# Loading and transposing 14 of 39 expert tiles in 32x32 blocks on VectorE instead of on TensorE

## What is computed

```
logits = x @ gate_w.T                       # 2048 rows, 8 experts
topk_w, topk_idx = top_k(softmax(logits), 2)   # then normalised to sum 1
h = einsum('th,ehi->eti', x, w1)            # 256 -> 176
g = einsum('th,ehi->eti', x, w3)
y_all = einsum('eti,eih->eth', silu(h) * g, w2)
y = sum of the two chosen experts' rows, weighted by topk_w
shared = silu(x @ sw1) * (x @ sw3) @ sw2    # 256 -> 352 -> 256, every row
```

## Time and profile before

| | us |
|---|---|
| median of 3 runs (lowest, highest) | 730.09 (728.05, 730.45) |
| the profiled execution | 729.91 |
| its span | 727.9 |
| TensorE busy, matmul | 716.8 |
| VectorE busy | 617.2 |
| ScalarE busy | 526.8 |
| GpSimd busy | 506.2 |
| clock granted to TensorE over the span | 0.998 |

### The profile page before, as it was taken

The page is one execution under the profiler, slowest core; times in us unless marked ns, Lnnn a source line. Parts: engine busy times, 40 slices in busy tenths (PEclk is TensorE's granted clock), DMA queues, the critical chain, the costliest instruction groups (busy, mean ns, idle before and its releaser), DMA issues.

```text
span 727.9 us, 16486 instructions
## 1 busy us (share of the span) xinstructions
PE 716.8 (98%) x5490; PEld 690.7 (95%) x5490; DVE 617.2 (85%) x1774; ACT 526.8 (72%) x1664; POOL 506.2 (70%) x531
## 2 busy tenths in 40 slices
PE   7999999999999999999999999999999999999997
PEld 6999999999999999999999999999999989999997
DVE  5888899989998999899989898989898976776657
ACT  5787777777777777777777777777777765666564
POOL 5898467787777777877777777777767623544545
PEclk9999999999999999999999999999999999999999
DMA  6555213221422143214321421131454373344383
GB/s 213 155 176 166 86 31 138 108 88 37 136 106 87 45 135 117 79 46 143 116 77 44 143 106 56 43 103 38 140 205 162 138 270 113 118 123 126 109 292 107
DMA packets 51211, 85.91 MB, mean 118 GB/s; under 512 B 8632, under 2 KB 43416, under 8 KB 49528
## 3 DMA queue, kind: packets, MB, share of 16 engines
q1 hardware_dynamic: 47080, 73.44, 30.3%
q0 software_dynamic: 4048, 11.42, 4.4%
HBM read 60.12 MB, written 44.59 MB: 144 GB/s over the span
## 4 chain that ended last, share of the span: by engine, by line
PE 80%; DVE 8%; POOL 6%; ACT 2%; issue 2%; DMA 1%; SPq 1%; POOLq 0%; DVEq 0%
PE bank L662 60%; PE bank L712 5%; PE bank L702 3%; PE bank L721 3%; POOL work L489 3%; DVE work L1104 2%; POOL rows_by_expert L1917 2%; DVE work L1097 1%; POOL qkt_lo L1788 1%; PE bank L954 1%; PE bank L935 1%; PE bank L704 1%; DVE xn L1261 1%; PE bank L849 1%; ACT work L1553 1%
## 5 line engine op out<-in xcount | busy, mean ns | idle before, releaser
L489 POOL TENSOR_TENSOR work<-work 128x512 f32<-128x512 f32 x127 | 164.9, 1298 | 52.7 <-DVE work L1104 51.9
L1788 POOL TENSOR_TENSOR qkt_lo<-work,qkt_hi 128x512 fp32r<-128x512 f32 x112 | 144.8, 1293 | 74.1 <-ACT qkt_hi L1546 74.1
L1104 DVE TENSOR_TENSOR work<-bank,sinn 64x512 f32<-64x512 f32 x256 | 176.2, 688 | 3.4
L662 PE MATMUL bank<-xnt_hi,w_lo 128*128 128x256 f32 x512 | 148.6, 290 | 0.8 <-DVE xnt_lo L1430 0.8
L662 PE MATMUL bank<-xnt_hi,w_hi 128*128 128x256 f32 x512 | 145.2, 284 | 0.0
L662 PE MATMUL bank<-xnt_lo,w_hi 128*128 128x256 f32 x512 | 145.2, 284 | 0.0
L1546 ACT CAST qkt_hi<-work 128x512 fp32r<-128x512 f32 x112 | 69.6, 622 | 87.3 <-POOL work L489 87.1
L1553 ACT ACTIVATE work<-work,bias 128x128 f32<-128x128 f32 (+1 forms) x256 | 112.7, 441 | 0.9 <-DVE bias L1113 0.9
L1097 DVE TENSOR_TENSOR work<-bank,cosn 128x512 f32<-128x512 f32 x128 | 88.0, 687 | 23.5 <-PE bank L662 23.2
L662 PEld LDWEIGHTS bank<-xnt_hi,w_lo 128*128 128x128 f32 x512 | 98.3, 192 | 1.7 <-DVE xnt_lo L1430 1.0
L662 PEld LDWEIGHTS bank<-xnt_hi,w_hi 128*128 128x128 f32 x512 | 98.6, 193 | 0.5
(11 more groups left out here) (205 smaller groups left out, 2125.3 us busy)
## 6 DMA issues: line engine op xcount, KB each, us to landing
rows_by_expert<-in_zero_t SPq DMA_DIRECT2D x17, 1028.0 KB
weights_split<-stage SPq DMA_DIRECT2D x40, 176.0 KB
w_lo<-weights_split SPq DMA_DIRECT2D x4, 1408.0 KB, 9.7
w_lo<-results_by_token SPq DMA_DIRECT2D x16, 256.0 KB, 5.3
w_lo<-rows_by_expert SPq DMA_DIRECT2D x24, 128.5 KB, 2.1
w_hi<-weights_split SPq DMA_DIRECT2D x2, 1536.0 KB, 6.4
stage<-in_L_ffn_w SPq DMA_DIRECT2D x32, 88.0 KB, 2.2
weights_split<-stage SPq DMA_DIRECT2D x20, 128.0 KB
```

Source lines behind the costliest of these rows:

```text
L489: eng.tensor_tensor(roped[:, a], rope_cos[:, a], rope_sin[:, a], ALU.add).then_inc(rope_add, 1)
L662: mm = pe.matmul(out, lhs[a], rhs[b], start=start and n == 0, stop=stop and n == 2, skip_group_check=more)
L1104: op = nc.vector.tensor_tensor(rope_sin[lo:lo + 64, a], p_qk[a][hi:hi + 64, :, :], sn, ALU.mult)
L1788: nc.gpsimd.tensor_tensor(qkt[a][1][:, :, :], roped[:, a], qkt[a][0][:, :, :], ALU.subtract).then_inc(qkt_lo, 1)
```

## The change

Fourteen tiles are marked in a list `BY_BLOCKS`: 5, 7, 9, 11, and of the tiles from 25 on those whose number is not a multiple of three: 25, 26, 28, 29, 31, 32, 34, 35, 37, 38.

A marked tile is loaded by five transfers instead of one: for each quarter q of the channels (64 of 256) one that puts the tile's rows, in four blocks of 32, on partitions 32q to 32q + 31 (128 pieces of 256 bytes), and one for the last word of each row (128 pieces of 4 bytes). VectorE then transposes the whole 128x256 slot in 32x32 blocks with one instruction into an SBUF buffer `x_turn`, in iteration j - 2, behind `low_x(j-1)`. For a marked tile TensorE has no `turn_x`, and `high_x` and `low_x` read `x_turn` in place of `p_xe`. `high_x` waits for `x_turned` and for `ue_ps` of tile j - 2.

For this the channels stand in another order in all tiles: channel 2s + c on partition s of piece c. The experts' w1 and w3 are loaded in that order (each partition's row is still 704 bytes), and the transposes that stay on TensorE read every second word of the slot.

```diff
@@ constants
+BY_BLOCKS = [j in (5, 7, 9, 11) or j >= NF + 4 and j % 3 > 0 for j in range(NJ)]
@@ buffers
+        x_turn = [work[:, 2560:2560 + D], work[:, 1728:1728 + D]]
+        QW = D // 4
+        def by_channel(row):
+            return row.rearrange("p (s c) -> p c s", c=DC)
+        def got_count(j):
+            return sum(80 if BY_BLOCKS[i] else 16 for i in range(j % ESLOTS, j + 1, ESLOTS))
@@ add_kept of w1 and w3
-                rc = slice(c * P, (c + 1) * P)
-                add_kept([(lambda t: t[:, 0:I], w1[e][rc]), (lambda t: t[:, I:UW], w3[e][rc])], UW,
+                gate, up = (t[e].rearrange("(p c) i -> c p i", c=DC)[c] for t in (w1, w3))
+                add_kept([(lambda t: t[:, 0:I], gate), (lambda t: t[:, I:UW], up)], UW,
@@ tile_in (SyncE)
-                sp.dma_start(x_slot[j % ESLOTS], xs_d[bass.ds(row, P), :]).then_inc(x_got[j % ESLOTS], 16)
+                if BY_BLOCKS[j]:
+                    for q in range(4):
+                        src = xs_d[bass.ds(row, P), q * QW:(q + 1) * QW].rearrange("(k i) s -> i k s", k=4)
+                        sp.dma_start(x_slot[j % ESLOTS][32 * q:32 * q + 32, 0:D].rearrange("p (k s) -> p k s", k=4),
+                                     src).then_inc(x_got[j % ESLOTS], 16)
+                    with nc.allow_non_contiguous_dma(reason="a word of each row"):
+                        sp.dma_start(x_slot[j % ESLOTS][:, D:RW], xs_d[bass.ds(row, P), D:RW]).then_inc(x_got[j % ESLOTS], 16)
+                else:
+                    sp.dma_start(x_slot[j % ESLOTS], xs_d[bass.ds(row, P), :]).then_inc(x_got[j % ESLOTS], 16)
@@ turn_x and its call (TensorE)
-                    mm = pe.transpose(p_xe[:, c, :], x_slot[j % ESLOTS][:, c * P:(c + 1) * P], ident[:, :])
+                    mm = pe.transpose(p_xe[:, c, :], by_channel(x_slot[j % ESLOTS][:, 0:D])[:, c], ident[:, :])
-                if j + 1 < NJ:
+                if j + 1 < NJ and not BY_BLOCKS[j + 1]:
                     turn_x(j + 1)
@@ VectorE
+            def turn_blocks(j):
+                dve.wait_ge(x_got[j % ESLOTS], got_count(j))
+                nc.vector.transpose(x_turn[j % 2].rearrange("p (c k i) -> p k c i", c=DC, k=4),
+                                    x_slot[j % ESLOTS][:, 0:D].rearrange("p (k s c) -> p k c s", k=4, c=DC)).then_inc(x_turned, 1)
             def low_x(j):
+                if BY_BLOCKS[j]:
+                    nc.vector.tensor_tensor(xe_t[1][:, j % 2], x_turn[j % 2].rearrange("p (c s) -> p c s", c=DC), xe_t[0][:, j % 2],
+                                            ALU.subtract).then_inc(xe_lo, 1)
                 if j + 1 < NJ:
                     low_x(j + 1)
+                if j + 2 < NJ and BY_BLOCKS[j + 2]:
+                    turn_blocks(j + 2)
@@ high_x (ScalarE)
+                if BY_BLOCKS[j]:
+                    act.wait_ge(x_turned, turned_by_dve(j))
+                    act.wait_ge(ue_ps, j - 1)
+                    nc.scalar.copy(xe_t[0][:, j % 2], x_turn[j % 2].rearrange("p (c s) -> p c s", c=DC)).then_inc(xe_hi, 1)
```

More of the change, by code:

```diff
@@ L192, in build, with turned_by_dve, turned_by_pe @@
         assert XSLOTS * TOP * D <= rows_at
+        x_turn = [work[:, 2560:2560 + D], work[:, 1728:1728 + D]]
[4 more added lines that the diff above has]
+            return sum(80 if BY_BLOCKS[i] else 16 for i in range(j % ESLOTS, j + 1, ESLOTS))
+        def turned_by_dve(j):
+            return sum(BY_BLOCKS[:j + 1])
+        def turned_by_pe(j):
+            return j + 1 - turned_by_dve(j)
         twin = work[:, DC * P:DC * P + ST * RW].rearrange("p (t d) -> p t d", t=ST)
@@ L336, in build @@
         xe_ps = sem("xe_ps")
+        x_turned = sem("x_turned")
         xe_hi = sem("xe_hi")
@@ L932, in turn_x @@
                     pe.wait_ge(xe_lo, j)
-                pe.wait_ge(x_got[j % ESLOTS], 16 * (j // ESLOTS + 1))
+                pe.wait_ge(x_got[j % ESLOTS], got_count(j))
                 for c in range(DC):
-                    mm = pe.transpose(p_xe[:, c, :], x_slot[j % ESLOTS][:, c * P:(c + 1) * P], ident[:, :])
+                    mm = pe.transpose(p_xe[:, c, :], by_channel(x_slot[j % ESLOTS][:, 0:D])[:, c], ident[:, :])
                 mm.then_inc(xe_ps, 1)
@@ L1320, in add_s @@
                 nc.vector.tensor_tensor(resid[:, t, :], resid[:, t, :], p_yy[t % 2][:, 0:D], ALU.add).then_inc(ys_add, 1)
+            def turn_blocks(j):
+                dve.wait_ge(x_got[j % ESLOTS], got_count(j))
+                nc.vector.transpose(x_turn[j % 2].rearrange("p (c k i) -> p k c i", c=DC, k=4),
+                                    x_slot[j % ESLOTS][:, 0:D].rearrange("p (k s c) -> p k c s", k=4, c=DC)).then_inc(x_turned, 1)
             def low_x(j):
                 dve.wait_ge(xe_hi, j + 1)
-                nc.vector.tensor_tensor(xe_t[1][:, j % 2], p_xe[:, 0:DC, :], xe_t[0][:, j % 2],
-                                        ALU.subtract).then_inc(xe_lo, 1)
+                if BY_BLOCKS[j]:
+                    nc.vector.tensor_tensor(xe_t[1][:, j % 2], x_turn[j % 2].rearrange("p (c s) -> p c s", c=DC), xe_t[0][:, j % 2],
+                                            ALU.subtract).then_inc(xe_lo, 1)
+                else:
+                    nc.vector.tensor_tensor(xe_t[1][:, j % 2], p_xe[:, 0:DC, :], xe_t[0][:, j % 2],
+                                            ALU.subtract).then_inc(xe_lo, 1)
             def mult_e(j):
@@ L1670, in high_x @@
             def high_x(j):
-                act.wait_ge(xe_ps, j + 1)
-                nc.scalar.copy(xe_t[0][:, j % 2], p_xe[:, 0:DC, :]).then_inc(xe_hi, 1)
+                if BY_BLOCKS[j]:
+                    act.wait_ge(x_turned, turned_by_dve(j))
+                    act.wait_ge(ue_ps, j - 1)
+                    nc.scalar.copy(xe_t[0][:, j % 2], x_turn[j % 2].rearrange("p (c s) -> p c s", c=DC)).then_inc(xe_hi, 1)
+                else:
+                    act.wait_ge(xe_ps, turned_by_pe(j))
+                    nc.scalar.copy(xe_t[0][:, j % 2], p_xe[:, 0:DC, :]).then_inc(xe_hi, 1)
             def silu_e(j):
```

## The result

| | before | changed |
|---|---|---|
| median (lowest to highest), 6 runs each | 729.10 (728.05 to 730.45) | 735.34 (733.95 to 736.26) |
| ratio, 95% interval | | 1.0087 (1.0074 to 1.0100) |
| span of the profiled execution | 727.9 | 734.2 |

What follows compares the result with a forecast made beforehand. TensorE's queue was taken to bound the expert stage, with SyncE becoming the late pace after the change. The early gain of 0.9 us and late loss of 1.4 made +0.5, so 730.4 us, range 728.4 to 732.2.

Steps and rivals of the forecast that it cites:

- TensorE's gain: Expert stage: each transpose taken from TensorE gives back about 0.22 us, fourteen of them 3.1 us.
- In the late stretch SyncE becomes the pace: Late expert tiles: three cost SyncE 6.23 us against TensorE's 5.55; the stage ends 1.4 us late; chance 0.52.
- the chain that it named: End of expert stage: last landing at 679.4, then VectorE's work until about 680.75, where TensorE wants it at 679.3.
- VectorE's terms: Transpose of a marked tile 0.45 us (0.29 to 0.69), fitting VectorE's queue; ScalarE's copy from SBUF 406 ns for 378, no cost.
- 13 steps of 0.81 and 10 x 4 of 0.475, 10.5 + 19.0 = 29.5 us: 677.3: SyncE's issues from tile 25's transfer at 647.76 to tile 38's last: 0.81 a tile, 0.475 each further transfer.
- the landing: Late stretch: the last transfer, issued at 677.3, was to take 2.1 us to land, at 679.4.
- The early four: Tiles 5 to 11: 7.6 us more on SyncE covered by the prefetch, so 0.9 us gained.
- SyncE costs more: Rival: each further transfer takes SyncE 0.55 us, so the 40 late ones add 3 us, 733.4 us; chance 0.18.
- The strided read: TensorE's 25 remaining transposes read every second word: taken as 0, at most 7 us; as rival 3.5, 733.9 us, chance 0.08.
- what the prediction said would show it right: Marked tiles 2.7 us on SyncE, no slot waits from tile 25, VectorE waiting for transfers, TensorE idle 3 to 4 us late.
- signs of being wrong: TensorE without idle time, longer weight loads on its transposes, or VectorE's transpose over 0.69 us with `mult_e` releasing TensorE.

Runs made afterwards that it cites:

- c: The changed kernel with each of the 14 marked tiles loaded by one plain transfer, so results are other numbers: 726.83 us, 0.9970 of the kernel before.
- k: The changed kernel, 12 slots, with only every third late tile from 25 to 37 marked, besides 5, 7, 9, 11: 729.57 us, 1.0010 of the kernel before.
- i: The changed kernel with 18 slots, marking odd tiles 5 to 19 and every third from 25 to 37: 727.74 us, 0.9986 of the kernel before.
- f: The changed kernel with 18 slots, marking every second tile from 5 to 19 and 25 to 37: 728.49 us, 0.9991 of the kernel before.

## Why the prediction was wrong

The mechanism and the place were right, its size was not. By its own steps:

- **TensorE's gain** was right: 0.23 us a tile (2.00 to 1.77), and c keeps it for the late ten. "In the late stretch SyncE becomes the pace" was right, and so was the chain that it named, landing, `turn_blocks(38)`, `mult_e(36)`, `low_e(35)`, `down_e(35)`.
- **VectorE's terms** were right. The transpose takes 0.446 us (0.45 taken), the copy from SBUF 407 ns (406), as these rows of the changed kernel show:

```profile
L1350 DVE STREAM_TRANSPOSE work<-w_lo x10: 431/446/446, 609.6 to 676.3; 128x256 f32<-128x256 f32 x10
...
L1711 ACT CAST qkt_hi<-work x14: 405/407/411, 611.3 to 684.6; 128x256 fp32r<-128x256 f32 x14
```

- **The step that failed** is "13 steps of 0.81 and 10 x 4 of 0.475, 10.5 + 19.0 = 29.5 us: 677.3". The last transfer is issued at 682.31. Of the 5.0 us, 0.6 is the later start (the scatter landed in 3.3 us, not 2.8), 1.5 is the spacing (2.86 for 2.71, ten times), and 2.9 is time that the sum had not at all: 2.2 in the two tiles with an issue of over a microsecond, 0.7 in the two with a pause between issues. Long issues had been in the trace of before: SyncE's go up to 1.6 us there in attention, where they cost little, with SyncE's queue at 1% of the chain. I took a median for each of 54 transfers in a row, and a row of 54 meets the tail. Against this the landing came 0.3 us sooner (1.8 for 2.1).
- **The early four** were put at 0.9 us, and by tile 20 there were 0.3: the plain transposes before it took part of it back by their strided reads, which the sum had at 0. So the scatter that frees tile 25's slot starts no sooner than before, at 644.61 us of its span where it was 644.52.
- **The rival "SyncE costs more"** had the direction. It was priced at 3.0 us through a spacing of 0.55, and 733.4. The spacing came to 0.50, a third of what was missed; the larger part was the long issues and pauses, which no rival named.
- **The strided read** was taken at 0 and is 0.02 to 0.03 us a plain tile, 0.5 to 0.8 for the 25. The Trainium skill's rule of two accesses to a line (SBUF — State Buffer, Door 1: The DMA port swizzle) would have it free; these weight loads take 204 ns for 142, so here the measurement decides against it.
- **The Trainium skill's sentence** on the issue time being "usually small relative to the DMA itself" (DMA: Bandwidth & Descriptors, Issuing engines are not separate DMA queues) does not hold in this stretch: 5 x 0.50 us of issue stand beside 1.8 of landing.
- Of what the prediction said would show it right, most is there, but larger: marked tiles near 2.7 (2.86), no more slot waits from tile 26 on, VectorE's waits before all ten late transposes, and TensorE's idle time, 2.9 us by 672 and 2.1 after it. One of its signs of being wrong is there too: the weight loads of the plain transposes are longer, 204 ns.

## What to carry to other kernels

A transfer split into five costs its queue five issues, so when an engine's work is traded for a different data layout, sum the issuing engine's queue over the stretch before the engine's own gain; compare it with the consumer's pace, and ask how far ahead it is when the stretch begins. A queue whose mean rate only just suffices can fail by its tail: leave it a margin of a long issue (here 1 to 2 us, an estimate from issues of 1.0 to 1.6). Here fewer late tiles alone (k) brought the loss of 6 us down to no difference, and fewer late tiles, more early ones and 18 slots together (i) to a gain of about 1.

## What was not expected of the hardware

Some issues of SyncE take 1.0 to 1.6 us instead of 0.32. In the changed kernel the two longest start at 659.65 and 676.74; in the half microseconds from 659.0 and from 676.5 the queue that brings instructions (q8) has one packet each. The transfers' rows of the first of these windows:

```profile
q8 instruction: 1, 0.02, 21.3%
```

In f the long ones at 646.24, 658.35 and 670.10 stand in the same way within 0.9 us of such a packet. But the packet of the half microsecond from 645.5 in the changed kernel has a plain transfer beside it at 645.55 that takes 0.33 us. In the kernel before these packets come every 11 to 14 us in the late stretch, where there is one plain transfer for every 2 us and all take 0.33. That the loading of instructions holds up the issue is what most of this suggests; no run here took it away, so it stays open. Transfers of 128 pieces of 256 or 4 bytes land in 1.8 us, quicker than 128 of 1028 bytes (2.1 to 2.2).
